# Output projection of the first attention: both row scalings on ScalarE, longer lags between the steps, the weight transposed inside the same stage

## The chip, the cores and the metric

The kernel runs on one core of a Trainium2 chip. The metric is the device time of one execution in microseconds (us). The core has five instruction streams that matter here: TensorE (PE: matmuls and transposes), VectorE (DVE), ScalarE (ACT), GpSimd (POOL) and SyncE (SP, which only issues DMAs here). Each runs its own list of instructions in order and waits for the others through semaphores. TensorE writes to PSUM; in this kernel GpSimd reads and writes SBUF alone.

## The reference, cut to what matters

Two transformer layers on an input of 2 x 1024 rows of 512. Each attention and each feed-forward is wrapped in the same way:

```python
def _layernorm(x, axis=-1, eps=1e-05):
    m = jnp.mean(x, axis=axis, keepdims=True)
    v = jnp.var(x, axis=axis, keepdims=True)
    return (x - m) / jnp.sqrt(v + eps)
...
    x = x + _layernorm(_L0_attn_ref(_layernorm(x, axis=-1), ...), axis=-1)
    x = x + _layernorm(_L0_ffn_ref(_layernorm(x, axis=-1), ...), axis=-1)
```

The change is at the end of the first attention. What is computed there, for 2048 rows: `y = out @ Wo.T` (the last line of the attention), `x1 = x0 + layernorm(y)`, and then `layernorm(x1)`, transposed, as the operand of the feed-forward.

## The kernel before

The program is a row of stages, and each stage is a block with one instruction list per engine and a barrier at its end. The stage in question, `project_residual_norm` (tiles named `l0o_...`), follows the attention (`l0a_...`) and a small stage of its own that transposes the weight Wo (`transpose_weights`, tiles `l0ot_...`). After it comes the first feed-forward (`f0f_...`).

`transpose_weights` takes Wo, already in SBUF (`raw`, shown as `l_raw`), through TensorE in 16 transposes of 128x128 (L133). ScalarE copies each of the four banks out, rounded to fp32r (the high part, L141), and VectorE writes the remainder (the low part, L151). High and low part together keep fp32's precision with three matmuls in place of one: high x high, high x low, low x high (`THREE`).

`project_residual_norm` then works on 16 tiles of 128 rows. For each tile t:

- ScalarE casts the attention's output to its high part (L403), and GpSimd subtracts to get the low part (L475).
- TensorE does y(t): 12 matmuls into a PSUM bank (L378), 4 blocks of the inner dimension times the three pairs.
- VectorE takes the row statistics of y (bn_stats L425, bn_aggr L430), ScalarE the square root (L397), VectorE the reciprocal (L435) and **the first row scaling**, (y - mean) * rstd, from PSUM to the tile z (L463).
- GpSimd adds the residual x0 (L482), and SyncE stores z as x1 (L362).
- VectorE takes the statistics of z, ScalarE the root, VectorE the reciprocal and **the second row scaling** from z to xn (L443).
- TensorE transposes xn in 4 pieces, below called T(t) (L386); ScalarE copies the bank out as the high part (L415) and VectorE the low part (L451), into `x_xT`, the operand of the feed-forward.

What sets the order is written out by hand: each engine runs a loop over steps i, and in step i it does each kind of work for the tile that lags by a fixed number. Before: T(i-5) and y(i) on TensorE; on VectorE second scaling of i-4, statistics of z of i-3, low part of i-6, statistics of y of i, first scaling of i-1. The rings `z`, `ybank`, `tbank` and `ot_hl` hold 4 tiles and `xn` holds 2, and waits guard their reuse. The Python loops are unrolled, so the program's order is the order in the code.

SyncE first issues two loads of x0 and six of the feed-forward's first weights, and then a store per tile.

Of the kernel before, what the change touches and what calls it, by code (L numbers as in the profile page):

```python
# [326 lines left out]
def project_residual_norm(nc, m, ident, tiles, src, dst, oT, WoT_hl, xT_hl, loads):  # L327
# [7 lines left out]
    xn = m.sb("xn", [P, 2, D])  # L335
    ot_hl = m.sb("ot_hl", [P, RING, 2, KT, P], F32R)
    stats, mv = m.sb("stats", [P, 2, RING, 6]), m.sb("mv", [P, 2, RING, 2])
    std, rstd = m.sb("std", [P, 2, RING]), m.sb("rstd", [P, 2, RING])
# [8 lines left out]
    stats_done, mv_done, std_done, rstd_done = ([m.sem(f"{n}{i}") for i in range(2)] for n in (  # L347
        "stats_done", "mv_done", "std_done", "rstd_done"))
    with nc.Block() as block:
# [20 lines left out]
        def _(pe):  # L370
            for i in range(tiles + 5):
# [19 lines left out]
        def _(act):  # L391
# [27 lines left out]
        @block.vector
        def _(dve):  # L420
            nc.vector.memset(eps[:, :], EPS_LN).then_inc(eps_set, 1)

# [9 lines left out]
            def inverse(which, t):  # L432
# [3 lines left out]
                dve.wait_ge(rstd_done[which], t + 1)  # L436

            for i in range(tiles + 6):
                if 0 <= i - 4 < tiles:
                    t, r = i - 4, (i - 4) % RING  # L440
                    inverse(1, t)
                    wait(dve, turned, t - 1)
                    nc.vector.tensor_scalar(xn[:, t % 2, :], z[:, r, :], mv[:, 1, r, 0:1], rstd[:, 1, r:r + 1],  # L443
                                            ALU.subtract, ALU.mult).then_inc(normed, 1)
                if 0 <= i - 3 < tiles:
                    dve.wait_ge(sum_done, i - 2)
                    statistics(1, i - 3, z[:, (i - 3) % RING, :])
                if 0 <= i - 6 < tiles:
                    t = i - 6
# [2020 lines left out]
```

## Time and profile before

| | us |
|---|---|
| median of 3 runs | 3204.28 |
| lowest and highest | 3202.85, 3204.48 |
| the profiled execution | 3199.93 |
| its span | 3198.2 |
| stage l0ot, first transpose to last low part | 632.75 to 637.74 |
| stage l0o, first matmul to last low part | 640.43 to 719.50 |

The profiled execution took 3199.93 us, of which the span of its instructions is 3198.2; it is 4.35 us below the median of the runs. The two stages take about 87 us of it, or 2.7%. All positions in the trace are in us from the span's start. A row of the timeline gives the start, the length, the engine and line, the operation with the tiles it writes and reads, how many of them are merged, and in brackets how long the engine had been idle and what ended that. An instruction of one engine can begin before the last has ended, so a loop's cost is read from start to start.

### The profile page before, as it was taken

How to read it: one execution, taken by the hardware profiler on the slowest of the kernel's cores; microseconds unless marked ns; L12 is line 12 of the kernel's file. 1: busy time of each engine (PE TensorE's matmuls, PEld its weight loads, DVE VectorE, ACT ScalarE, POOL GpSimd, SP SyncE). 2: the span in 40 equal slices, each digit the busy share in tenths (PEclk: the TensorE clock that was granted, in tenths of full speed). 3: DMA queues.
4: the chain of work that ended last, by engine and by line, in shares of the span. 5: the costliest groups of instructions: out<-in, count | busy, mean ns of one | idle time of the engine just before them, and what ended most of it. 6: DMA issues, size and time to landing. Idle time of an engine off the chain costs nothing. (4 is left out here: it accounts for less than half of the span.)

```text
span 3198.2 us, 42777 instructions
## 1 busy us (share of the span) xinstructions
PE 2861.6 (89%) x14636; PEld 2287.2 (72%) x14636; DVE 1894.0 (59%) x3604; ACT 1210.8 (38%) x2334; POOL 992.9 (31%) x780
## 2 busy tenths in 40 slices
PE   7969999779999999458899999857999999499998
PEld 5846666557787878347788888746888888378886
DVE  5647788584453545445566666655666666654446
ACT  2226666532221212133344444322444444243334
POOL 1217877655554636304100000033000000122223
PEclk9979999889999999779999999979999999799999
DMA  4774444142121201671100000040000000300012
GB/s 163 241 210 143 120 128 130 39 144 80 47 63 41 64 24 35 203 283 70 40 23 23 34 23 34 10 159 29 24 23 34 23 23 30 125 20 21 10 36 79
DMA packets 138034, 244.06 MB, mean 76 GB/s; under 512 B 14416, under 2 KB 78928, under 8 KB 137392
## 3 DMA queue, kind: packets, MB, share of 16 engines
q1 hardware_dynamic: 137904, 242.40, 23.2%
q8 instruction: 73, 1.20, 0.2%
q14 instruction: 57, 0.47, 0.0%
HBM read 162.92 MB, written 79.17 MB: 76 GB/s over the span
## 5 line engine op out<-in xcount | busy, mean ns | idle before, releaser
L1071 POOL TENSOR_TENSOR l0a_probs_hl<-l0a_probs,l0a_probs_hl 128x896 fp32r<-128x896 f32 (+1 forms) x128 | 285.3, 2249 | 107.3 <-ACT l0a_probs L999 107.3
L1329 ACT ACTIVATE l1a_probs<-l1a_scores,l1a_row 128x128 f32<-128x128 f32 (+7 forms) x256 | 189.7, 742 | 317.4 <-DVE l1a_row L1366 317.4
L1303 PE MATMUL l1a_obank<-l1a_pT_hl,l1k_v_hl 128*128 128x512 f32 (+3 forms) x1152 | 300.2, 369 | 7.1 <-DVE l1a_pT_hl L1376 7.1
L1376 DVE TENSOR_TENSOR l1a_pT_hl<-l1a_work,l1a_pT_hl 128x512 fp32r<-128x512 f32 (+3 forms) x384 | 213.1, 555 | 154.4 <-ACT l1a_pT_hl L1336 154.2
L1419 POOL TENSOR_TENSOR l1a_q_stage<-l1k_qpe,l1a_ones 128x512 fp32r<-128x512 f32 x32 | 33.4, 1043 | 872.4 <-PE l1a_work L1311 816.7
L1283 PE MATMUL l1a_scores<-l1k_kT_hl,l1a_qa_hl 128*128 128x512 f32 (+3 forms) x1152 | 291.1, 361 | 1.5 <-ACT l1a_probs L1329 1.5
L1336 ACT CAST l1a_pT_hl<-l1a_work 128x512 fp32r<-128x512 f32 (+3 forms) x384 | 183.7, 478 | 105.7 <-PE l1a_work L1294 104.5
L1311 PE MATMUL l1a_work<-l1a_wov,l1a_oT_hl 128*128 128x512 f32 x768 | 214.2, 401 | 5.0 <-DVE l1a_oT_hl L1395 3.0
L1366 DVE TENSOR_REDUCE l1a_row<-l1a_scores 128x1 f32<-128x128 f32 (+7 forms) x256 | 189.8, 751 | 44.0 <-PE l1a_scores L1286 43.9
L1390 DVE SCALAR_TENSOR_TENSOR l_acc<-l1a_work,l1a_row,l_acc 128x512 f32<-128x512 f32 x256 | 189.4, 750 | 34.1 <-PE l1a_work L1311 24.5
L1690 PE MATMUL f0f_ybank<-f0f_wT,f0f_h_hl 128*128 128x512 f32 x768 | 196.5, 406 | 12.6 <-POOL f0f_h_hl L1856 12.5
L1283 PEld LDWEIGHTS l1a_scores<-l1k_kT_hl,l1a_qa_hl 128*128 128x128 f32 x1152 | 188.1, 190 | 21.7 <-ACT l1a_probs L1329 1.8
L1283 PE MATMUL l1a_scores<-l1k_kpe,l1a_q_stack 128*128 128x512 f32 (+3 forms) x768 | 203.1, 346 | 0.0
L1303 PEld LDWEIGHTS l1a_obank<-l1a_pT_hl,l1k_v_hl 128*128 128x128 f32 x1152 | 181.4, 191 | 28.8 <-DVE l1a_pT_hl L1376 14.8
L1294 PE MATMUL l1a_work<-all_ident,l1a_probs 128*128 128x128 f32 x1152 | 191.8, 275 | 9.5 <-DVE l1a_qa_hl L1381 6.1
L1680 PE MATMUL f0f_gbank<-x_xT,f0f_wT 128*128 128x512 f32 x768 | 192.1, 399 | 1.4 <-DVE f0f_wT L1761 1.4
L1680 PE MATMUL f0f_ubank<-x_xT,f0f_wT 128*128 128x512 f32 x768 | 189.3, 395 | 0.0
L1767 DVE TENSOR_TENSOR f0f_hid<-f0f_silu,f0f_ubank 128x512 f32<-128x512 f32 x64 | 44.0, 688 | 229.4 <-PE f0f_ubank L1680 207.4
L1690 PEld LDWEIGHTS f0f_ybank<-f0f_wT,f0f_h_hl 128*128 128x128 f32 x768 | 145.2, 194 | 44.4 <-issue 9.2
L998 ACT ACTIVATE l0a_probs_hl<-l0a_sbank 128x896 fp32r<-128x896 f32 (+1 forms) x128 | 124.5, 972 | 135.3 <-PE l0a_sbank L964 77.9
L1294 PEld LDWEIGHTS l1a_work<-all_ident,l1a_probs 128*128 128x128 f32 x1152 | 140.3, 140 | 47.8 <-DVE l1a_qa_hl L1381 12.8
L1680 PEld LDWEIGHTS f0f_gbank<-x_xT,f0f_wT 128*128 128x128 f32 x768 | 145.8, 190 | 36.7 <-DVE f0f_wT L1761 1.6
(254 smaller groups left out, 6191.0 us busy)
## 6 DMA issues: line engine op xcount, KB each, us to landing
v_dram<-l0f_v_rows SPq DMA_DIRECT2D x24, 768.0 KB, 4.0
qk_dram<-l0f_stage SPq DMA_DIRECT2D x128, 128.0 KB, 2.5
l1a_wov<-wov_dram SPq DMA_DIRECT2D x32, 512.0 KB, 3.4
l0a_v_stage<-v_dram SPq DMA_DIRECT2D x32, 384.0 KB, 4.3
l1a_wabs<-wabs_dram SPq DMA_DIRECT2D x32, 384.0 KB, 3.9
l0a_q_stack<-qk_dram SPq DMA_DIRECT2D x32, 256.0 KB, 3.6
l0a_k_stack<-qk_dram SPq DMA_DIRECT2D x32, 256.0 KB, 3.9
f0f_chunk<-in_L_ffn_w_gate_up SPq DMA_DIRECT2D x32, 256.0 KB, 2.7
```

Source lines behind the costliest of these rows:

```text
L1071: nc.gpsimd.tensor_tensor(probs_hl[:, r, 1, 0:wide], probs[:, r, 0:wide], f32(probs_hl[:, r, 0, 0:wide]), ALU.subtract).then_inc(low_done, 1)
L1283: last = pe.matmul(scores[:, buf, cols], lhs, rhs, start=(i == 0), stop=(not diagonal and i == len(steps) - 1))
L1294: last = pe.transpose(work[:, slot, i * P:(i + 1) * P], probs[s][:, first + n, :], ident[:, :])
L1303: last = pe.matmul(obank[:, c:SPAN], src["v_hl"][:, a, n, :], pT_hl[:, ring(n, s), b, c:SPAN], start=(n == 0 and i == 0), stop=(n == QT * ...
L1311: last = pe.matmul(work[:, slot, :], oT_hl[:, s, a, n * P:(n + 1) * P], wov[:, hp, b, :], start=(i == 0), stop=(i == 2))
L1329: nc.scalar.activation(probs[s][:, first:first + wide, :].rearrange("p k c -> p (k c)"), scores[:, n % S_AHEAD, 0:wide * P], ACT.Exp, bias ...
L1336: nc.scalar.copy(pT_hl[:, ring(n, s), 0, c:SPAN], work[:, slot, c:SPAN]).then_inc(turned_high, 1)
L1366: nc.vector.tensor_reduce(row[:, 0, row_slot:row_slot + 1], scores[:, n % S_AHEAD, 0:wide * P], AX.X, ALU.max, negate=True).then_inc(max_d ...
L1376: nc.vector.tensor_tensor(pT_hl[:, r, 1, c:SPAN], work[:, slot, c:SPAN], f32(pT_hl[:, r, 0, c:SPAN]), ALU.subtract).then_inc(work_free[slo ...
L1390: nc.vector.scalar_tensor_tensor(out=out[:, t, :], in0=work[:, slot, :], scalar=row[:, 2, row_slot:row_slot + 1], in1=out[:, t, :], op0=AL ...
L1680: last = pe.matmul(bank[:, b, :], wT[:, half, wa, w, c * HG + b * P:c * HG + (b + 1) * P], xT_hl[:, xa, c, a * SPAN:(a + 1) * SPAN], start ...
L1690: last = pe.matmul(ybank[:, b % 2, :], h_hl[:, a % 2, ht, ha, b * P:(b + 1) * P], wT[:, half, wa, 2, ht * D:(ht + 1) * D], start=(n == 0), ...
```

## The change

- The stage `l0ot` is gone. Its 16 transposes, 4 casts and 4 subtractions stand at the begin of `l0o`, behind the first three casts of the attention's output on ScalarE. They use the first four uses of `tbank`, which is why the counts of `turned`, `high_done` and `low_done` start at `KT` (4). The weight's tile moves from `l_WoT` to `l0o_WoT_hl`.
- Both row scalings are now ScalarE's, as `Identity(scale * in + bias)` with scale = rstd and bias = -mean * rstd. For that bias VectorE computes a `shift` (128x1) after each reciprocal.
- The lags are longer: T(i-7) in place of T(i-5); the low part of xT at i-9 in place of i-6; the residual sum at i-2 in place of i-1; the second scaling at i-6 in place of i-4.

```diff
@@ class of work on TensorE @@
+            for k in range(KT):
+                for o in range(KT):
+                    last = pe.transpose(tbank[:, k, o * P:(o + 1) * P], raw[:, o, k * P:(k + 1) * P], ident[:, :])
+                last.then_inc(turned, 1)
+            pe.wait_ge(low_done, KT)
-            for i in range(tiles + 5):
+            for i in range(tiles + 7):
...
-                if i >= 5:
-                    t = i - 5
+                if i >= 7:
+                    t = i - 7
                     pe.wait_ge(normed, t + 1)
-                    wait(pe, low_done, t - RING + 1)
+                    pe.wait_ge(low_done, KT + t - RING + 1)
@@ ScalarE @@
+            def scaled(which, t, to, rows):
+                r = t % RING
+                act.wait_ge(shift_done[which], t + 1)
+                return nc.scalar.activation(to, rows, ACT.Identity, bias=shift[:, which, r:r + 1],
+                                            scale=rstd[:, which, r:r + 1])
...
+            for k in range(KT):
+                act.wait_ge(turned, k + 1)
+                nc.scalar.copy(WoT_hl[:, 0, k, :], tbank[:, k, :]).then_inc(high_done, 1)
+            for i in range(tiles + 8):
+                if 0 <= i - 5 < tiles:
+                    root(1, i - 5)
                 if 0 <= i - 1 < tiles:
                     root(0, i - 1)
                 if 0 <= i - 6 < tiles:
                     t = i - 6
-                    act.wait_ge(turned, t + 1)
+                    act.wait_ge(turned, KT + t - 1)
+                    scaled(1, t, xn[:, t % 2, :], z[:, t % RING, :]).then_inc(normed, 1)
+                if 0 <= i - 8 < tiles:
+                    t = i - 8
+                    act.wait_ge(turned, KT + t + 1)
                     nc.scalar.copy(xT_hl[:, 0, :, t * P:(t + 1) * P],
...
+                if 0 <= i - 2 < tiles:
+                    t, r = i - 2, (i - 2) % RING
+                    wait(act, stored[r], 16 * (t // RING))
+                    wait(act, normed, t - RING + 1)
+                    scaled(0, t, z[:, r, :], ybank[:, r, :]).then_inc(z_done, 1)
                 high(i + 3)
@@ VectorE @@
+            for i in range(tiles + 9):
+                if 0 <= i - 5 < tiles:
+                    inverse(1, i - 5)
...
+                    statistics(1, i - 4, z[:, (i - 4) % RING, :])
+                if i < tiles:
+                    dve.wait_ge(y_full, i + 1)
+                    statistics(0, i, ybank[:, i % RING, :])
+                if 0 <= i - 4 < tiles:
+                    aggregate(1, i - 4)
+                if 0 <= i - 1 < tiles:
+                    inverse(0, i - 1)
+                if 0 <= i - 9 < tiles:
...
                 if i < tiles:
                     aggregate(0, i)
@@ GpSimd @@
-                if 0 <= i - 1 < tiles:
-                    t = i - 1
+                if 0 <= i - 2 < tiles:
+                    t = i - 2
```

VectorE's list, one tile in the middle of the stage, before (L443 is the second scaling, L463 the first, L451 the low part of xT):

```order
L443 TENSOR_SCALAR l0o_xn<-l0o_z,l0o_mv,l0o_rstd 128x512
L425 BN_STATS l0o_stats<-l0o_z 128x6
L451 TENSOR_TENSOR x_xT<-l0o_tbank,x_xT 128x4x128
L430 BN_AGGR l0o_mv<-l0o_stats 128x2
L425 BN_STATS l0o_stats<-l0o_ybank 128x6
L435 RECIPROCAL l0o_rstd<-l0o_std 128x1
L463 TENSOR_SCALAR l0o_z<-l0o_ybank,l0o_mv,l0o_rstd 128x512
L430 BN_AGGR l0o_mv<-l0o_stats 128x2
L435 RECIPROCAL l0o_rstd<-l0o_std 128x1
```

VectorE's list, one tile in the middle of the stage, of the changed kernel (L465 is the new shift):

```order
L463 RECIPROCAL l0o_rstd<-l0o_std 128x1
L465 SCALAR_TENSOR_TENSOR l0o_shift<-l0o_mv,l0o_rstd 128x1
L453 BN_STATS l0o_stats<-l0o_z 128x6
L453 BN_STATS l0o_stats<-l0o_ybank 128x6
L458 BN_AGGR l0o_mv<-l0o_stats 128x2
L463 RECIPROCAL l0o_rstd<-l0o_std 128x1
L465 SCALAR_TENSOR_TENSOR l0o_shift<-l0o_mv,l0o_rstd 128x1
L485 TENSOR_TENSOR x_xT<-l0o_tbank,x_xT 128x4x128
L458 BN_AGGR l0o_mv<-l0o_stats 128x2
```

The two operations on 128x512 are gone from it and two on 128x1 have come; the low part of xT stands late in the step.

ScalarE's list, one tile in the middle of the stage, before (two roots, the copy of xT, the cast of the next attention tile):

```order
L397 ACTIVATE l0o_std<-l0o_mv,l0o_eps 128x1 x2
L415 CAST x_xT<-l0o_tbank 128x4x128
L403 CAST l0o_ot_hl<-l_oT 128x512
L397 ACTIVATE l0o_std<-l0o_mv,l0o_eps 128x1 x2
L415 CAST x_xT<-l0o_tbank 128x4x128
```

ScalarE's list of the changed kernel, the same place:

```order
L403 ACTIVATE l0o_std<-l0o_mv,l0o_eps 128x1 x2
L409 ACTIVATE l0o_xn<-l0o_z,l0o_shift,l0o_rstd 128x512
L434 CAST x_xT<-l0o_tbank 128x4x128
L409 ACTIVATE l0o_z<-l0o_ybank,l0o_shift,l0o_rstd 128x512
L415 CAST l0o_ot_hl<-l_oT 128x512
```

Both scalings stand between the roots and the cast for tile i+3, one on each side of the copy of xT.

The begin of the changed stage on ScalarE, up to the first scaling:

```order
L415 CAST l0o_ot_hl<-l_oT 128x512 x3
L421 CAST l0o_WoT_hl<-l0o_tbank 128x512 x4
L415 CAST l0o_ot_hl<-l_oT 128x512
L403 ACT_TABLE_LOAD
L403 ACTIVATE l0o_std<-l0o_mv,l0o_eps 128x1
L415 CAST l0o_ot_hl<-l_oT 128x512
L403 ACTIVATE l0o_std<-l0o_mv,l0o_eps 128x1
L409 ACTIVATE l0o_z<-l0o_ybank,l0o_shift,l0o_rstd 128x512
```

The weight's four casts stand behind three of the attention's output, in the same block; the load of the activation table (ACT_TABLE_LOAD) is the only one of the stage, as it was before.

## Rows read from the trace of the kernel before

**Rows 1.** Busy time in two stretches; the first row names the columns.
```profile
core 0: us, PE busy (x) PEld busy (x) DVE busy (x) ACT busy (x) POOL busy (x), PEclk, DMA share, GB/s
642.00:643.00 1.00, 1.00 (x4) 0.80 (x3) 0.00 (x0) 0.00 (x0) 1.00 (x2) 0.50 1.00 352
700.00:720.00 20.00, 5.45 (x23) 3.37 (x21) 17.86 (x38) 5.49 (x14) 3.79 (x3) 0.62 0.14 52
```

**Rows 2.** Waits, 640 to 720: total us, times, longest.
```profile
PE l0o_tbank L386 <- DVE l0o_xn L443: 15.0, 13, 3.7
PE l0o_ybank L378 <- POOL l0o_ot_hl L475: 7.5, 9, 4.0
```

**Rows 3.** Timeline of VectorE, one tile: start, length, operation.
```profile
667.12 1.48 DVE L443 TENSOR_SCALAR l0o_xn<-l0o_z,l0o_mv,l0o_rstd 128x512 f32<-128x512 f32 x1
668.52 0.68 DVE L425 BATCH_NORM_STATS2 l0o_stats<-l0o_z 128x6 f32<-128x512 f32 x1
669.12 0.67 DVE L451 TENSOR_TENSOR x_xT<-l0o_tbank,x_xT 128x512 fp32r<-128x512 f32 x1
669.71 0.17 DVE L430 BATCH_NORM_AGGREGATE l0o_mv<-l0o_stats 128x2 f32<-128x6 f32 x1
669.80 0.66 DVE L425 BATCH_NORM_STATS2 l0o_stats<-l0o_ybank 128x6 f32<-128x512 f32 x1
670.38 0.14 DVE L435 RECIPROCAL l0o_rstd<-l0o_std 128x1 f32<-128x1 f32 x1
670.56 0.81 DVE L463 TENSOR_SCALAR l0o_z<-l0o_ybank,l0o_mv,l0o_rstd 128x512 f32<-128x512 f32 x1
671.29 0.17 DVE L430 BATCH_NORM_AGGREGATE l0o_mv<-l0o_stats 128x2 f32<-128x6 f32 x1
...
671.55 1.48 DVE L443 TENSOR_SCALAR l0o_xn<-l0o_z,l0o_mv,l0o_rstd 128x512 f32<-128x512 f32 x1
```

**Rows 4.** Timeline: the second scaling with GpSimd idle; four casts of GpSimd with VectorE idle.
```profile
716.44 0.55 DVE L443 TENSOR_SCALAR l0o_xn<-l0o_z,l0o_mv,l0o_rstd 128x512 f32<-128x512 f32 x1
...
639.11 4.99 POOL L475 TENSOR_TENSOR l0o_ot_hl<-l_oT,l0o_ot_hl 128x512 fp32r<-128x512 f32 x4 [6.87 <-ACT l0o_ot_hl L403]
```

**Rows 5.** Timeline of TensorE: the weight's transposes, the first y, a step, y(15).
```profile
632.75 3.65 PE L133 MATMUL l0ot_bank<-all_ident,l_raw 128*128 128x128 f32 x16 [12.67 <-PEq L836]
640.43 17.93 PE L378 MATMUL l0o_ybank<-l_WoT,l0o_ot_hl 128*128 128x512 f32 x72 [4.03 <-POOL l0o_ot_hl L475]
...
661.39 0.60 PE L386 MATMUL l0o_tbank<-all_ident,l0o_xn 128*128 128x128 f32 x4
661.74 3.02 PE L378 MATMUL l0o_ybank<-l_WoT,l0o_ot_hl 128*128 128x512 f32 x12
664.60 0.60 PE L386 MATMUL l0o_tbank<-all_ident,l0o_xn 128*128 128x128 f32 x4
...
696.38 3.02 PE L378 MATMUL l0o_ybank<-l_WoT,l0o_ot_hl 128*128 128x512 f32 x12 [0.47 <-POOL l0o_ot_hl L475]
```

**Rows 6.** Timeline of ScalarE: a step here, and the same Identity in the last stage.
```profile
675.93 0.29 ACT L397 ACTIVATE l0o_std<-l0o_mv,l0o_eps 128x1 f32<-128x1 f32 x1 [1.29 <-DVE l0o_mv L430]
676.14 0.57 ACT L415 CAST x_xT<-l0o_tbank 128x512 fp32r<-128x512 f32 x1
676.60 0.62 ACT L403 CAST l0o_ot_hl<-l_oT 128x512 fp32r<-128x512 f32 x1
...
3183.09 0.30 ACT L1734 ACTIVATE f1f_root<-f1f_var,f1f_eps 128x4 f32<-128x4 f32 x1 [0.58 <-DVE f1f_var L1812]
3183.82 2.94 ACT L1739 ACTIVATE f1f_z<-f_acc,f1f_shift,f1f_rstd 128x512 f32<-128x512 f32 x4 [0.44 <-DVE f1f_shift L1820]
```

**Rows 7.** Timeline of VectorE: last weight low part, last of xT, a shift elsewhere.
```profile
637.05 0.69 DVE L151 TENSOR_TENSOR l_WoT<-l0ot_bank,l_WoT 128x512 fp32r<-128x512 f32 x1 [0.16 <-ACT l_WoT L141]
...
718.81 0.69 DVE L451 TENSOR_TENSOR x_xT<-l0o_tbank,x_xT 128x512 fp32r<-128x512 f32 x1 [0.63 <-ACT x_xT L415]
...
3190.48 0.16 DVE L1820 SCALAR_TENSOR_TENSOR f1f_shift<-f1f_mv,f1f_rstd 128x4 f32<-128x4 f32 x1
```

More of the change, by code:

```diff
@@ L324, in _, with project_residual_norm @@
                 nc.gpsimd.tensor_tensor(z[:, r, :], z[:, r, :], x[:, t % (2 * QT), :], ALU.add).then_inc(sum_done, 1)
-def project_residual_norm(nc, m, ident, tiles, src, dst, oT, WoT_hl, xT_hl, loads):
+def project_residual_norm(nc, m, ident, tiles, src, dst, oT, raw, xT_hl, loads):
     RING = 4
@@ L335, in project_residual_norm @@
     xn = m.sb("xn", [P, 2, D])
+    WoT_hl = m.sb("WoT_hl", [P, 2, KT, D], F32R)
     ot_hl = m.sb("ot_hl", [P, RING, 2, KT, P], F32R)
     stats, mv = m.sb("stats", [P, 2, RING, 6]), m.sb("mv", [P, 2, RING, 2])
-    std, rstd = m.sb("std", [P, 2, RING]), m.sb("rstd", [P, 2, RING])
+    std, rstd, shift = (m.sb(n, [P, 2, RING]) for n in ("std", "rstd", "shift"))
     eps = m.sb("eps", [P, 1])
@@ L406, in _ @@
                 high(t)
-            for i in range(tiles + 6):
-                if 0 <= i - 4 < tiles:
-                    root(1, i - 4)
+            for k in range(KT):
[4 more added lines that the diff above has]
+                    root(1, i - 5)
                 if 0 <= i - 1 < tiles:
@@ L421, in _ @@
             nc.vector.memset(eps[:, :], EPS_LN).then_inc(eps_set, 1)
+            for k in range(KT):
+                dve.wait_ge(high_done, k + 1)
+                nc.vector.tensor_tensor(WoT_hl[:, 1, k, :], tbank[:, k, :], f32(WoT_hl[:, 0, k, :]), ALU.subtract
+                                        ).then_inc(low_done, 1)
             def statistics(which, t, y):
@@ L436, in inverse @@
                 dve.wait_ge(rstd_done[which], t + 1)
-            for i in range(tiles + 6):
-                if 0 <= i - 4 < tiles:
[L440 to L449, printed above, removed]
-                    dve.wait_ge(high_done, t + 1)
+                nc.vector.scalar_tensor_tensor(out=shift[:, which, r:r + 1], in0=mv[:, which, r, 0:1], scalar=-1.0,
+                                               in1=rstd[:, which, r:r + 1], op0=ALU.mult, op1=ALU.mult
+                                               ).then_inc(shift_done[which], 1)
+            for i in range(tiles + 9):
+                if 0 <= i - 5 < tiles:
+                    inverse(1, i - 5)
+                if 0 <= i - 4 < tiles:
+                    dve.wait_ge(sum_done, i - 3)
+                    statistics(1, i - 4, z[:, (i - 4) % RING, :])
[7 more added lines that the diff above has]
+                if 0 <= i - 9 < tiles:
+                    t = i - 9
+                    dve.wait_ge(high_done, KT + t + 1)
                     nc.vector.tensor_tensor(xT_hl[:, 1, :, t * P:(t + 1) * P],
@@ L453, in _ @@
                                             f32(xT_hl[:, 0, :, t * P:(t + 1) * P]), ALU.subtract).then_inc(low_done, 1)
-                if 0 <= i - 3 < tiles:
-                    aggregate(1, i - 3)
-                if i < tiles:
-                    dve.wait_ge(y_full, i + 1)
-                    statistics(0, i, ybank[:, i % RING, :])
-                if 0 <= i - 1 < tiles:
-                    t, r = i - 1, (i - 1) % RING
-                    inverse(0, t)
-                    wait(dve, stored[r], 16 * (t // RING))
-                    nc.vector.tensor_scalar(z[:, r, :], ybank[:, r, :], mv[:, 0, r, 0:1], rstd[:, 0, r:r + 1],
-                                            ALU.subtract, ALU.mult).then_inc(z_done, 1)
                 if i < tiles:
                     aggregate(0, i)
-            dve.wait_ge(low_done, tiles)
+            dve.wait_ge(low_done, KT + tiles)
         @block.gpsimd
         def _(pool):
-            for i in range(-2, tiles + 1):
+            for i in range(-2, tiles + 2):
                 if i + 2 < tiles:
```

10 lines of the change are left out of this document (3 added, 7 removed).

## Prediction

> **What bounds the kernel now.** The page's slices say that TensorE is the busiest engine of the whole, so I first asked whether it is so in the stage that is changed. The waits of that stretch say no: TensorE waits 15.0 us for the second scaling and 7.5 us for the low part of the attention's output [rows 2]. VectorE's timeline shows why: one tile takes 671.55 - 667.12 = 4.43 us, with no idle time in any row [rows 3]. TensorE's own step, where nothing held it, is 664.60 - 661.39 = 3.21 us: 0.35 for a T and 2.86 for a y [rows 5]. So VectorE sets the pace here and TensorE is next. Three stretches are to be read separately: the begin (last transpose of the weight to the first matmul), the sixteen y, and the tail, from the end of y(15) at 696.38 + 3.02 = 699.40 to the last low part at 718.81 + 0.69 = 719.50. The tail is 20.1 us in which TensorE does only small transposes (5.45 us busy of 20) and VectorE is nearly full (17.86) [rows 1].
>
> **The begin.** The 16 transposes still start when the attention ends, near 632.75, and take 3.65 us [rows 5]; nothing of the new stage lets them start earlier. In the way of ScalarE stand three casts of 0.62 [rows 6], together 1.9 us, which end near 634.6; the fourth bank is only full at 636.4, so the last weight cast is not moved, nor the last low part, which ends at 637.05 + 0.69 = 637.74 [rows 7]. TensorE can then start y(0), near 637.8, since GpSimd has made its low part (1.25 us [rows 4]) by about 635. Before, y(0) started at 640.43 [rows 5], because a barrier, a cast and a GpSimd pass stood in between. Gain: **2.6 us**. SyncE's eight loads start some 5 us earlier, beside nothing else. The clock: before, TensorE had run its first matmuls at a granted 0.50, which is 1.2 GHz, and still at 642 to 643 [rows 1], 2.6 us from the first, worth 1.3 us. After, its pause is 1.4 us and not 4.0. I assume the same slow start; if the clock is up sooner, up to 1.3 us more.
>
> **The pace.** Per tile, from start to start:
>
> VectorE keeps two statistics (0.60 and 0.58), the low part (0.59), two aggregates (0.09 each), two reciprocals (0.18 each) [rows 3]: 2.31. It gains two shifts. The nearest row is one of 128x4, 0.16 [rows 7]; with overlap 0.1, at most 0.18. Sum 2.5 (at most 2.7). What leaves is 1.40 and 0.73, less the 0.2 for the shifts.
>
> ScalarE keeps two roots (0.21), the copy of xT (0.46), and the cast (0.62, say 0.55 where another follows) [rows 6]. It gains two Identities. The trace has the very instruction in the last stage: four in 2.94 us, or (2.94 - 0.80) / 3 = 0.71 from start to start, 0.80 alone [rows 6]. It reads SBUF there, while one of the two reads PSUM here; copies cost 0.57 from PSUM and 0.62 from SBUF, so I take 0.80 for both. Sum: 0.42 + 1.42 + 0.46 + 0.55 = **2.85**. Without any overlap: 0.58 + 1.60 + 0.57 + 0.62 = 3.37. There is no new table load: in the last stage a root is followed by Identities with none in between [rows 6], and the changed list has a single one.
>
> GpSimd: a cast at 1.25 (4.99 for four [rows 4]) and a sum of the same shape, taken alike: 2.5, far from the bound too.
>
> The second scaling takes 1.48 while GpSimd works and 0.55 when it doesn't [rows 3, 4], so the move frees more of VectorE than it costs ScalarE. The Trainium skill speaks against the move: in "ScalarE: Activation LUTs", section "Rules for kernel authors", adding and multiplying belong on VectorE, which it calls up to about 3 times faster in bf16. By the row with GpSimd idle that would hold (0.55 against 0.80), by the row beside GpSimd it doesn't; and a rule for one operation doesn't say which engine sets the pace.
>
> So TensorE is next, at 3.21. Do the new waits let it run? Call Y(i) the end of y(i). VectorE ends its step i about 1.9 behind Y(i) (statistics, reciprocal and shift, low part, two aggregates). ScalarE's step i+1 begins there and takes 2.65 more from its second root, to Y(i) + 4.5. TensorE needs z free for y(i+3) (the scaling of tile i-1, done by Y(i) + 4), which is due at Y(i) + 6.4 or later, and xn of tile i-5 for the T behind y(i+2), due at Y(i) + 6.4, done at Y(i) + 3. Each has over 2 us to spare. The steps of VectorE and ScalarE depend on each other over two steps: ScalarE 2.65, a root 0.35, VectorE 2.5, in all 5.5 for two tiles, 2.75 for one. TensorE holds.
>
> The sixteen y: the first six as before, 17.93 (with the slow clock); y(6) and y(7) at 2.86; eight steps of 3.21 for the rest. Sum 17.9 + 5.7 + 25.7 = 49.3, in place of 699.40 - 640.43 = 58.97. Gain: **9.7 us**. With ScalarE at 3.37 for the last eight it is 1.3 less.
>
> **The tail.** Followed for tile 15, from its y full: VectorE's step 1.8; ScalarE root, Identity, copy, Identity of tile 14 (2.1), then root, Identity, copy (1.4): the first scaling of tile 15 begins at 5.3 and ends at 6.1. GpSimd's sum to 7.4. VectorE is in a low part until 8.4; statistics and aggregate to 9.2. Root; the Identity of tile 14 and a copy (1.4); VectorE's reciprocal and shift lie beside them. The second scaling of tile 15 begins at 10.6 and ends at 11.4; four transposes at the slow clock, about 1.1, to 12.5; copy 0.6, low part 0.7: **14.0 us**. Gain 20.1 - 14.0 = **6.1 us**. The longer lags add no time of their own, because a step without y is cheap. With no overlap of neighbours each piece grows by a tenth or two, some 2 us less gain; if ScalarE reaches tile 15 earlier than I let it, 1.5 more.
>
> **Sum.** 2.6 + 9.7 + 6.1 = 18.4 us. The profiled execution goes from 3199.93 to 3181.5. The median of the runs stands 4.35 above it, and I carry that over: 3204.28 - 18.4 = 3185.9. The next stage is only moved: its weights are issued at the begin of this stage and are there long before.
>
> **Rivals.**
>
> *ScalarE becomes the bound.* Its list grows from under half full to 89% (2.85 of 3.21), with six waits in a step. For it: the nearest rows leave 0.36 a tile. Against: most semaphores are long up. At 3.6 a tile over the ten tiles from y(6) on, the pace loses 10 x 0.39 = 3.9 of its gain and keeps 5.8; the tail keeps 4.5: with the begin 12.9 us, 3191.4.
>
> *The clock is up early.* 1.3 us more: 3184.6.
>
> *Lockstep, slower than before.* ScalarE's root for tile i-1 waits for the last instruction of VectorE's step i-1, and VectorE's step i begins with a wait for a root. If the two took turns rather than ran beside each other, a tile would take 2.85 + 2.5 = 5.35; sixteen, 85.6 us in place of 59, a loss of 27, less 2.6 and what is left of the tail's gain: about +20, 3224. It decides from about (59 + 2.6 + 6.1) / 16 = 4.2 a tile. Against it: the roots stand first in ScalarE's step, so VectorE is released while ScalarE's long part runs.
>
> *The gain is given back.* The next stage would have to wait for something that doesn't move, such as a weight load. SyncE issues those before the tiles, so there is next to nothing for it. Result within 6 us of before.
>
> **Chances.** TensorE's pace with a clock as before: 0.70. ScalarE the bound: 0.14. Clock early: 0.08. Given back: 0.05. Lockstep: 0.03. The measurement tells a difference of about 0.2%, 6.4 us. Faster 0.92, same 0.05, slower 0.03. The range reaches from the early clock and a tail shorter by 1.5 with a us for the scatter of the runs (3182) to the case with ScalarE as the bound and half a us of scatter (3192).
>
> **What would show it.** Right: y(0) near 637.8; T to T 3.2 us with TensorE without a wait in the middle; VectorE idle a fifth of each tile; Identity 0.80 or less; last low part near 701. If the second scaling was slow because of GpSimd, GpSimd's casts in the middle of the stage take what they take at its begin with VectorE idle, 1.25 [rows 4]. (The Trainium skill, "SBUF — State Buffer", section "Who interferes with whom", names one exclusive pair of ports for the two engines; no term above needs it.) **Wrong:** T to T of 3.5 with TensorE waiting for xn or z (ScalarE), over 4.2 (lockstep), Identity from PSUM well over 0.8, a tail over 16, or y(0) at 640.

## The result, and the profile after

The changed kernel took 3187.83 us in the median of 5 runs (3182.02 to 3191.39), the kernel before 3204.28 (3202.57 to 3207.29 in 5). The medians lie 16.5 us or 0.5% apart. The ratio on record is 0.9941, with a 95% interval of 0.9930 to 0.9952, which is 15 to 22 us faster. The forecast was 3185.9, in a range of 3182 to 3192. The interval holds both the 18.4 us that were forecast and the 16.5 of the medians, so the whole time can't tell them apart.

The profiled execution took 3187.83 us with a span of 3186.0, 12.2 us below that of before; 18.4 was forecast against that one. Where the two meet and differ is read in the stage. TensorE's timeline of the changed kernel, to be held against [rows 5]:

```profile
633.10 3.65 PE L374 MATMUL l0o_tbank<-all_ident,l_raw 128*128 128x128 f32 x16 [12.79 <-PEq L859]
638.15 23.77 PE L384 MATMUL l0o_ybank<-l0o_WoT_hl,l0o_ot_hl 128*128 128x512 f32 x96 [1.40 <-DVE l0o_WoT_hl L448]
...
668.18 0.60 PE L392 MATMUL l0o_tbank<-all_ident,l0o_xn 128*128 128x128 f32 x4
668.53 3.00 PE L384 MATMUL l0o_ybank<-l0o_WoT_hl,l0o_ot_hl 128*128 128x512 f32 x12
671.38 0.60 PE L392 MATMUL l0o_tbank<-all_ident,l0o_xn 128*128 128x128 f32 x4
...
684.84 3.02 PE L384 MATMUL l0o_ybank<-l0o_WoT_hl,l0o_ot_hl 128*128 128x512 f32 x12
```

y(0) stands 638.15 - 633.10 = 5.05 us behind the first transpose (7.68 before). From T to T it is 3.20 us, with no wait in brackets: TensorE sets the pace. (One step of the eight, from 674.59 to 678.08, took 3.49.) y(15) ends at 687.86. VectorE's last low parts (three merged) end at 703.06:

```profile
701.05 2.01 DVE L485 TENSOR_TENSOR x_xT<-l0o_tbank,x_xT 128x512 fp32r<-128x512 f32 x3 [0.50 <-ACT x_xT L434]
```

| us | before | forecast | after |
|---|---|---|---|
| begin, first transpose to y(0) | 7.68 | 5.1 | 5.05 |
| the sixteen y | 58.97 | 49.3 | 49.71 |
| tail, y(15) to the last low part | 20.10 | 14.0 | 15.20 |
| stage | 86.75 | 68.4 | 69.96 |

The stage gave 16.8 us of the 18.4 forecast. What is short, 1.6 us, is in the y and the tail. VectorE's timeline shows an instruction that I had priced at 0.16 us; GpSimd's timeline of the same moment follows it.

```profile
667.35 0.12 DVE L463 RECIPROCAL l0o_rstd<-l0o_std 128x1 f32<-128x1 f32 x1
667.51 1.05 DVE L465 SCALAR_TENSOR_TENSOR l0o_shift<-l0o_mv,l0o_rstd 128x1 f32<-128x1 f32 x1
668.49 0.17 DVE L458 BATCH_NORM_AGGREGATE l0o_mv<-l0o_stats 128x2 f32<-128x6 f32 x1
668.58 0.12 DVE L463 RECIPROCAL l0o_rstd<-l0o_std 128x1 f32<-128x1 f32 x1
668.74 1.08 DVE L465 SCALAR_TENSOR_TENSOR l0o_shift<-l0o_mv,l0o_rstd 128x1 f32<-128x1 f32 x1
```

```profile
667.25 1.29 POOL L505 TENSOR_TENSOR l0o_z<-l0o_z,l0o_x 128x512 f32<-128x512 f32 x1 [1.13 <-ACT l0o_z L409]
668.50 1.29 POOL L498 TENSOR_TENSOR l0o_ot_hl<-l_oT,l0o_ot_hl 128x512 fp32r<-128x512 f32 x1
```

The shift, one element per row, takes 1.05 and 1.08 us. Its ends, 668.56 and 669.82, lie 0.02 and 0.03 behind the ends of GpSimd's instructions, 668.54 and 669.79. Reciprocals of the same size beside the same GpSimd work take 0.12. Of the 32 shifts 20 started while GpSimd was at work, and all of them end within 0.03 us of the end of its instruction; the 12 that met it idle took 0.16. The groups of the stage, ordered by cost (busy us and mean ns behind the bar), put it together:

```profile
L505 POOL TENSOR_TENSOR l0o_z<-l0o_z,l0o_x 128x512 f32<-128x512 f32 x16 | 20.5, 1284 | 15.6 <-ACT l0o_z L409 15.6
L498 POOL TENSOR_TENSOR l0o_ot_hl<-l_oT,l0o_ot_hl 128x512 fp32r<-128x512 f32 x16 | 20.5, 1289 | 7.1 <-ACT l0o_ot_hl L415 7.1
L465 DVE SCALAR_TENSOR_TENSOR l0o_shift<-l0o_mv,l0o_rstd 128x1 f32<-128x1 f32 x32 | 17.6, 551 | 1.1
L409 ACT ACTIVATE l0o_xn<-l0o_z,l0o_shift,l0o_rstd 128x512 f32<-128x512 f32 x16 | 12.8, 801 | 0.0
L409 ACT ACTIVATE l0o_z<-l0o_ybank,l0o_shift,l0o_rstd 128x512 f32<-128x512 f32 x16 | 12.4, 775 | 0.2
```

Thirty-two shifts cost 17.6 us of VectorE's time in place of 5. GpSimd's casts and sums are at 1.29 each, or 1.25 from start to start, as at the begin of the stage (the casts in the middle were near 1.45 before), and the Identities at 0.80 from SBUF and 0.78 from PSUM.

### The profile page after: what moved, and what is told of

Its sections match the earlier page's. It is cut to its first block and busy times, and to the rows that moved or that the text cites. A ratio compares the mean times of both kernels' runs of the same rounds, so it can differ in the third digit from the quotient of the medians.

```text
span 3186.0 us, 42804 instructions
## 1 busy us (share of the span) xinstructions
PE 2862.2 (90%) x14636; PEld 2289.0 (72%) x14636; DVE 1879.3 (59%) x3604; ACT 1231.7 (39%) x2366; POOL 990.2 (31%) x780
```

## The experiments

Each stage time below is read as in the table above, from the first transpose of the weight to the last low part of xT, in the profiled execution; it depends little on the rest of the kernel, unlike the whole time. Whole times are medians, and ratios are against the kernel before, run on the same chip. One thing differs between the profiles that the edits don't explain: in four of the twelve (the lags alone, the scalings alone, only the second scaling, the reciprocal later) TensorE's granted clock was already 1.00 at the first y; in the others it was at half then and came up later. Here are the four and then, for comparison, the changed kernel and the run with only the first scaling, each in a stretch of 1 us early in the first y.

```profile
639.00:640.00 1.00, 1.00 (x6) 0.82 (x5) 0.00 (x0) 0.60 (x1) 0.66 (x1) 1.00 1.06 383
636.00:637.00 1.00, 1.00 (x6) 0.83 (x5) 0.00 (x0) 0.18 (x1) 0.24 (x1) 1.00 1.03 389
637.00:638.00 1.00, 1.00 (x5) 0.84 (x5) 0.00 (x0) 0.84 (x1) 0.91 (x1) 1.00 1.04 406
637.00:638.00 1.00, 1.00 (x6) 0.77 (x6) 0.00 (x0) 0.47 (x1) 0.53 (x1) 1.00 1.01 381
```

```profile
639.00:640.00 1.00, 1.00 (x3) 0.73 (x3) 0.00 (x0) 0.19 (x1) 0.24 (x1) 0.50 0.94 313
637.00:638.00 1.00, 1.00 (x4) 0.71 (x4) 0.00 (x0) 0.59 (x1) 0.64 (x1) 0.50 0.97 356
```

The granted clock is third from the end. In all twelve it was up before the first y was full, so what it costs lies ahead of VectorE's statistics: VectorE's first statistics of y start 3.0 to 3.1 us behind the start of y(0) in the four and 4.4 to 5.3 in the others. So stage times are compared across the two groups from those first statistics to the last low part; a table at the end of this section has both lengths.

**The weight alone.** The kernel before with the transposes, casts and subtractions of the weight at the begin of the stage.

```diff
+            for k in range(KT):
+                for o in range(KT):
+                    last = pe.transpose(tbank[:, k, o * P:(o + 1) * P], raw[:, o, k * P:(k + 1) * P], ident[:, :])
+                last.then_inc(turned, 1)
+            pe.wait_ge(low_done, KT)
             for i in range(tiles + 5):
...
-                with phase("l0ot") as m:
-                    transpose_weights(nc, m, ident, square_jobs(raw, WoT, 0, -1), [])
```

> The kernel before with one edit: the weight is transposed inside the projection's stage; scalings and lags as before. My theory: the begin is worth the 2.6 us that the trace of after shows between the first transpose and y(0) (7.68 to 5.05) and nothing else changes: VectorE stays at 4.43 us a tile, the stage goes from 86.8 us (first transpose of the weight to last low part) to 84.1, the time falls by 2 to 3 us. Rival: the earlier begin is taken back, because VectorE sets the pace: then the stage stays near 86.8.

Begin 5.05, y 59.12, tail 20.14: stage 84.31, so 2.4 us less. The time was 3202.06 (before 3202.50), ratio 0.9994 (0.9984 to 1.0004), which tells no difference of this size. The begin gives its own length and nothing else; VectorE's pace is the old one.

**Everything but the weight.** The changed kernel with the weight in its own stage.

```diff
-            for k in range(KT):
-                for o in range(KT):
-                    last = pe.transpose(tbank[:, k, o * P:(o + 1) * P], raw[:, o, k * P:(k + 1) * P], ident[:, :])
-                last.then_inc(turned, 1)
-            pe.wait_ge(low_done, KT)
...
+                with phase("l0ot") as m:
+                    transpose_weights(nc, m, ident, square_jobs(raw, WoT, 0, -1), [])
```

> The changed kernel with the weight transposed in its own stage as before; scalings on ScalarE and long lags kept. If the parts add up, the two stages together take 70.0 + 2.6 = 72.6 us, y(0) starts 7.7 us after the first transpose, the sixteen y take 49 to 50 us and the tail 15; time 14 us below before. If the early begin matters for more than itself (clock, loads), the sum is off by 1.5 us or more.

Begin 7.67, y 49.96, tail 15.23: 72.86, within 0.3 of the sum of parts. From the first statistics it takes 60.18 us, and the changed kernel 60.16. The time was 3190.37, ratio 0.9952 (0.9939 to 0.9965). The parts add up.

**The lags alone.** The changed kernel with both scalings on VectorE, at the changed kernel's lags. The order inside VectorE's step is the changed kernel's too, with the low part of xT late in it, so this run changes lags and order together.

```diff
                 if 0 <= i - 5 < tiles:
                     inverse(1, i - 5)
+                if 0 <= i - 6 < tiles:
+                    t, r = i - 6, (i - 6) % RING
+                    dve.wait_ge(turned, KT + t - 1)
+                    nc.vector.tensor_scalar(xn[:, t % 2, :], z[:, r, :], mv[:, 1, r, 0:1], rstd[:, 1, r:r + 1],
+                                            ALU.subtract, ALU.mult).then_inc(normed, 1)
...
                 if 0 <= i - 1 < tiles:
                     inverse(0, i - 1)
+                if 0 <= i - 2 < tiles:
+                    t, r = i - 2, (i - 2) % RING
...
+                    nc.vector.tensor_scalar(z[:, r, :], ybank[:, r, :], mv[:, 0, r, 0:1], rstd[:, 0, r:r + 1],
+                                            ALU.subtract, ALU.mult).then_inc(z_done, 1)
```

> The changed kernel (weight inside the stage, long lags) with both scalings back on VectorE at the same lags, and no shift. My theory: VectorE sets the pace as before, 4.2 to 4.5 us a tile from T to T, TensorE waits for VectorE's results; stage 83 to 90 us. Rival: the longer lags alone brought the pace, by taking waits out: 3.2 to 3.5 a tile and a stage near 70.

My theory missed: 3.83 us from T to T and a stage of 77.44 (begin 5.05, y 52.14, tail 20.25); 3196.07, ratio 0.9976 (0.9966 to 0.9986). VectorE still sets the pace, as its timeline of this run shows, but the second scaling takes 0.89 there and not 1.48. Below it is GpSimd's, and then the sum of GpSimd that the scaling at 667.12 of the kernel before met.

```profile
675.23 0.81 DVE L479 TENSOR_SCALAR l0o_z<-l0o_ybank,l0o_mv,l0o_rstd 128x512 f32<-128x512 f32 x1
675.96 0.69 DVE L484 TENSOR_TENSOR x_xT<-l0o_tbank,x_xT 128x512 fp32r<-128x512 f32 x1
676.55 0.18 DVE L449 BATCH_NORM_AGGREGATE l0o_mv<-l0o_stats 128x2 f32<-128x6 f32 x1
676.64 0.14 DVE L454 RECIPROCAL l0o_rstd<-l0o_std 128x1 f32<-128x1 f32 x1
676.81 0.89 DVE L463 TENSOR_SCALAR l0o_xn<-l0o_z,l0o_mv,l0o_rstd 128x512 f32<-128x512 f32 x1
```

```profile
676.12 1.29 POOL L504 TENSOR_TENSOR l0o_z<-l0o_z,l0o_x 128x512 f32<-128x512 f32 x1 [1.10 <-DVE l0o_z L479]
677.37 1.49 POOL L497 TENSOR_TENSOR l0o_ot_hl<-l_oT,l0o_ot_hl 128x512 fp32r<-128x512 f32 x1
```

```profile
667.03 1.29 POOL L482 TENSOR_TENSOR l0o_z<-l0o_z,l0o_x 128x512 f32<-128x512 f32 x1 [1.70 <-DVE l0o_z L463]
```

Before, the scaling of xn followed 0.18 us behind the end of the scaling of z, which starts GpSimd's sum, so it met nearly the whole sum [rows 3]. In this order a low part lies between them, and 0.6 us of the sum is left when it starts. The run shows this inside itself. Its first four second scalings stand before the first low part of xT, directly behind the first scaling, and take 1.48 to 1.49; from the fifth on a low part lies between, and they take 0.88 or 0.89 for as long as there are y:

```profile
668.56 1.48 DVE L463 TENSOR_SCALAR l0o_xn<-l0o_z,l0o_mv,l0o_rstd 128x512 f32<-128x512 f32 x1
...
672.13 0.68 DVE L484 TENSOR_TENSOR x_xT<-l0o_tbank,x_xT 128x512 fp32r<-128x512 f32 x1
...
672.99 0.88 DVE L463 TENSOR_SCALAR l0o_xn<-l0o_z,l0o_mv,l0o_rstd 128x512 f32<-128x512 f32 x1
```

VectorE's step stays at 3.83 us as the low part comes in: its 0.60 is what the scaling no longer waits. So the 0.6 us that a tile gained against the 4.43 before come from the place of the low part in VectorE's step. What the longer lags add with the scalings on VectorE wasn't measured apart from that.

**The scalings alone.** The changed kernel, weight inside, with the lags of before. The low part stays late in VectorE's step.

```diff
-                if 0 <= i - 6 < tiles:
-                    t = i - 6
+                if 0 <= i - 4 < tiles:
+                    t = i - 4
                     act.wait_ge(turned, KT + t - 1)
                     scaled(1, t, xn[:, t % 2, :], z[:, t % RING, :]).then_inc(normed, 1)
...
-                if 0 <= i - 2 < tiles:
-                    t, r = i - 2, (i - 2) % RING
+                if 0 <= i - 1 < tiles:
+                    t, r = i - 1, (i - 1) % RING
```

> The changed kernel (weight inside, scalings on ScalarE) with the lags of before: T(i-5), low part at i-6, sum at i-1, second scaling at i-4, first scaling at i-1. My theory: ScalarE's first scaling of i-1 then waits for a shift that VectorE makes near the end of its own step, and VectorE's next step waits for a root that stands behind it: the two engines take turns, 4.2 to 4.7 us a tile, stage 82 to 90 us, no better than with the weight alone. Rival: the lags don't matter, 3.2 a tile, and fewer steps in the tail make the stage 67 to 70 us.

3.80 us from T to T, stage 77.04 (begin 5.04, y 53.45, tail 18.55); 3190.17, ratio 0.9957 (0.9941 to 0.9972). The mechanism is there, the size was too large. The waits between 655 and 690 of this run (total us, times, longest) show that ScalarE and VectorE wait for each other in each tile:

```profile
POOL l0o_z L505 <- ACT l0o_z L409: 11.5, 9, 1.3
DVE l0o_rstd L463 <- ACT l0o_std L403: 8.5, 9, 1.5
PEld l0o_tbank L392 <- ACT l0o_xn L409: 7.3, 9, 0.8
ACT l0o_xn L409 <- DVE l0o_shift L465: 5.8, 9, 1.1
PE l0o_tbank L392 <- ACT l0o_xn L409: 3.5, 9, 0.4
ACT l0o_z L409 <- DVE l0o_shift L465: 3.1, 10, 0.7
```

So neither of the two gives the pace of 3.2 alone. Read from the first statistics, the 74.7 us of the weight alone become 69.3 with the lags (and the new order) and 68.9 with the scalings, so each alone is worth 5.4 to 5.8 us, and together they are worth 14.5, more than their sum. Between this run and the changed kernel, with the order the same, the longer lags are worth 68.9 - 60.2 = 8.7 us. (The stage times 77.4 and 77.0 flatter both by the 1.5 us of the early clock.)

**One scaling each.** The changed kernel with only the second scaling on ScalarE, and with only the first; the other is on VectorE, in the form of the run with the lags alone.

```diff
@@ only the second on ScalarE @@
...
-                    scaled(0, t, z[:, r, :], ybank[:, r, :]).then_inc(z_done, 1)
...
+                if which != 1:
+                    return
...
@@ only the first on ScalarE @@
...
-                    scaled(1, t, xn[:, t % 2, :], z[:, t % RING, :]).then_inc(normed, 1)
...
+                if which != 0:
+                    return
...
```

> The changed kernel with only the second scaling (xn) on ScalarE; the first (z from PSUM, 0.81 us) is on VectorE at the same lag, and one shift is left. VectorE: 2.31 + 0.73 + a shift of 0.1 to 0.9 = 3.1 to 3.9 a tile. Theory: the second scaling was the one worth moving, as it was held by GpSimd: pace 3.2 to 3.5 (lags alone gave 3.83), stage 70 to 75. Rival: both moves are needed, pace above 3.6.

> The changed kernel with only the first scaling (z) on ScalarE; the second (xn) is on VectorE and one shift is left. VectorE: 2.31 + 0.55 to 1.40 + a shift of 0.1 to 0.9 = 3.0 to 4.6 a tile. Theory: 3.5 to 4.0 a tile, close to the 3.83 of the lags alone, because the shift and the scaling both wait for GpSimd; stage 75 to 79. Rival: the two moves are worth the same, and this one runs at the pace of the other.

Only the second: 3.56 from T to T, stage 74.29, 3189.43 (ratio 0.9957, 0.9941 to 0.9973). Only the first: 3.2 up to T(4) and 3.6 to 4.1 behind it, stage 76.30, 3190.24 (0.9963, 0.9950 to 0.9975). Both stages lie in the ranges expected, the first near its upper end (its pace of 3.56 is just above the 3.5), the second near its lower. But they can't be compared as they stand, since the clock was up early in the first and not in the second. From the first statistics they take 66.26 and 66.34 us, against 69.33 with both scalings on VectorE and 60.16 with none. So each move alone is worth about 3 us, and both 9.2: for the whole stage the rival that I had put to the second run, that the two moves are worth the same, holds. In the steady part the second is worth more (3.56 a tile against 3.77); the first makes up for it before T(4). The single shift left waits as well, 0.62 us in the median in the one and 0.89 in the other.

**GpSimd's sum in one column.** The kernel before, where GpSimd adds the residual in the first column alone.

```diff
-                    nc.gpsimd.tensor_tensor(z[:, r, :], z[:, r, :], x[:, t % (2 * QT), :], ALU.add).then_inc(sum_done, 1)
+                    nc.gpsimd.tensor_tensor(z[:, r, 0:1], z[:, r, 0:1], x[:, t % (2 * QT), 0:1], ALU.add
+                                            ).then_inc(sum_done, 1)
```

> The kernel before with one edit that changes what is computed: GpSimd adds the residual x0 in the first of the 512 columns alone, so its sum is short (x1 and all that follows lack x0 in the others). Theory: the second scaling on VectorE took 1.48 us in the stage because GpSimd's sum ran beside it; with the sum gone it takes 0.54 to 0.7 where GpSimd is idle, VectorE's step falls from 4.43 to 3.5 to 3.7, and the y take 52 to 54 us. Rival: the 1.48 is the price of that instruction in this place (its operands or the one before it), and it stays over 1.3.

The y took 60.30 us where I expected 52 to 54, and the one execution 3196.97 us. I had asked for the scaling to be fast "where GpSimd is idle" and overlooked that GpSimd isn't: its next cast moves up into the gap. VectorE's row, then GpSimd's:

```profile
681.02 1.60 DVE L443 TENSOR_SCALAR l0o_xn<-l0o_z,l0o_mv,l0o_rstd 128x512 f32<-128x512 f32 x1
```

```profile
681.07 1.27 POOL L475 TENSOR_TENSOR l0o_ot_hl<-l_oT,l0o_ot_hl 128x512 fp32r<-128x512 f32 x1
```

The scaling started 0.05 us ahead of the cast and ended 0.28 behind its end (682.62 against 682.34). In the middle of the stage the step even grew, to 4.55 us from T to T. (Another 0.9 us of the y stand before T(0), where TensorE's clock was at half for longer.) But the casts end with tile 15, and then neither of GpSimd's large instructions is left: VectorE still does both scalings and takes 3.49 us for a step (T at 696.32, 699.80, 703.29), where it took 4.40 before, and the second scaling takes 0.55:

```profile
699.20 0.55 DVE L443 TENSOR_SCALAR l0o_xn<-l0o_z,l0o_mv,l0o_rstd 128x512 f32<-128x512 f32 x1
```

Before, GpSimd's sum still ran there, so this pair has one difference. The 0.9 us is GpSimd's; the scaling waits for whichever of GpSimd's instructions it meets.

**The shift in another form.** The changed kernel with a tensor_scalar, which takes rstd as a per-row scalar and reads one tensor.

```diff
-                nc.vector.scalar_tensor_tensor(out=shift[:, which, r:r + 1], in0=mv[:, which, r, 0:1], scalar=-1.0,
-                                               in1=rstd[:, which, r:r + 1], op0=ALU.mult, op1=ALU.mult
-                                               ).then_inc(shift_done[which], 1)
+                nc.vector.tensor_scalar(shift[:, which, r:r + 1], mv[:, which, r, 0:1], rstd[:, which, r:r + 1], -1.0,
+                                        ALU.mult, ALU.mult).then_inc(shift_done[which], 1)
```

> The changed kernel with the shift computed by a tensor_scalar (mean times the per-row scalar rstd times -1: one tensor read from SBUF) in place of the scalar_tensor_tensor, which reads two. In the trace of after that one took 551 ns in the mean (up to 1.17 us), and its end falls on the end of a GpSimd instruction. Theory A: an instruction of VectorE with two inputs from SBUF waits for GpSimd's running one; then the mean falls to 0.13 to 0.20 us, VectorE's step to 2.5 us, TensorE's pace stays 3.21 (it sets it), the 0.3 us stall in the middle goes, the tail falls from 15.2 to 14.0 to 14.6; stage 68.4 to 69.2 us, time 1 us below after. Theory B: every VectorE instruction that follows a reciprocal there is held: the mean stays near 0.5 and nothing changes.

The row of the tile (least, median and most ns) is without a wait in any of the 32:

```profile
L465 DVE TENSOR_SCALAR l0o_shift<-l0o_mv,l0o_rstd x32: 212/214/216, 647.3 to 698.3; 128x1 f32<-128x1 f32 x32
```

Alone it is dearer than the old form (0.21 against 0.16), and it is never held. Begin 5.05, y 49.22, tail 13.91: stage 68.18. 3186.19, ratio 0.9944 (0.9930 to 0.9958), not to be told from the changed kernel by the whole time; the stage is 1.8 us shorter, 1.6 of it behind the first statistics and 0.2 in the clock before them. Between 662 and 688 VectorE was busy for 20.00 us of 26, and in the changed kernel for 25.15:

```profile
662.00:688.00 26.00, 26.00 (x131) 21.49 (x130) 20.00 (x71) 22.17 (x47) 18.95 (x15) 1.00 0.41 142
```

```profile
662.00:688.00 26.00, 25.95 (x131) 21.24 (x130) 25.15 (x72) 21.63 (x46) 19.39 (x16) 1.00 0.38 135
```

Theory A holds, with one thing left open: the edit changes the operation and the number of its inputs from SBUF at once. That two inputs alone are not enough the low part of xT shows, a tensor_tensor with one input in PSUM and one in SBUF, which takes 0.66 to 0.69 us in the changed kernel whether GpSimd works beside it or not.

**The reciprocal later.** On top of that, VectorE's step with the second scaling's reciprocal behind the aggregate.

```diff
             for i in range(tiles + 9):
-                if 0 <= i - 5 < tiles:
-                    inverse(1, i - 5)
...
                 if 0 <= i - 4 < tiles:
                     aggregate(1, i - 4)
+                if 0 <= i - 5 < tiles:
+                    inverse(1, i - 5)
```

> As the run with the tensor_scalar shift, and in VectorE's step the reciprocal and shift of the second scaling stand behind the statistics and aggregate of z rather than before them. In the tail of after, a step takes 2.0 us, as a root, a reciprocal, a shift, the statistics, an aggregate and the next root stand in one chain. Without the first three in it a step is 1.5 to 1.7: tail 12.5 to 13.5 us, stage 67 to 68 us, time 1.5 to 3 us below after. If ScalarE's own list (root, Identity, copy: 1.4) or the sum of z bounds the tail instead, nothing beyond the shift's part is gained.

Begin 4.84, y 47.72, tail 13.66: stage 66.22; 3184.90, ratio 0.9944 (0.9930 to 0.9958). The tail is only 0.25 us shorter, above the 12.5 to 13.5 expected: the other case of the expectation holds, that ScalarE's own list bounds it. ScalarE's timeline shows no wait in it: a step with an Identity for z takes 2.03 us and one without 1.37, and that list is now the bound.

```profile
688.58 0.80 ACT L409 ACTIVATE l0o_xn<-l0o_z,l0o_shift,l0o_rstd 128x512 f32<-128x512 f32 x1
689.29 0.57 ACT L434 CAST x_xT<-l0o_tbank 128x512 fp32r<-128x512 f32 x1
689.75 0.78 ACT L409 ACTIVATE l0o_z<-l0o_ybank,l0o_shift,l0o_rstd 128x512 f32<-128x512 f32 x1
690.43 0.29 ACT L403 ACTIVATE l0o_std<-l0o_mv,l0o_eps 128x1 f32<-128x1 f32 x1
690.61 0.81 ACT L409 ACTIVATE l0o_xn<-l0o_z,l0o_shift,l0o_rstd 128x512 f32<-128x512 f32 x1
```

The other 1.5 us, in the y, aren't the edit's (from the first statistics the two runs take 58.28 and 58.55). Busy time in stretches of 1 us, with the granted clock third from the end: the first y of this run, and then the first of the changed kernel.

```profile
636.00:637.00 1.00, 0.52 (x2) 0.47 (x3) 0.43 (x1) 0.98 (x2) 0.96 (x2) 1.00 1.02 363
```

```profile
640.00:641.00 1.00, 1.00 (x4) 0.78 (x3) 0.00 (x0) 0.00 (x0) 0.00 (x0) 0.50 1.05 408
641.00:642.00 1.00, 1.00 (x4) 0.77 (x3) 0.00 (x0) 0.00 (x0) 0.00 (x0) 0.59 1.08 412
```

The instructions up to there are the same in both, and the clock was up (1.00, 2.4 GHz) at the first y in one execution and at half for over 3 us in the other. That is the rival of the early clock, worth 1.5 us. Nine kernels of the study have the same instructions up to the first y, with the weight inside the stage; in the one profile that there is of each, four had the clock up and five had it at half for another 3.1 to 4.0 us. So it is not a property of one kernel, and why an execution falls on one side stays open.

**Two scalings back in the tail.** On top of that, the first scaling of tiles 14 and 15 at the end of VectorE's step.

```diff
...
+                if tiles - 2 <= i - 1 < tiles:
+                    t, r = i - 1, (i - 1) % RING
+                    wait(dve, stored[r], 16 * (t // RING))
+                    wait(dve, normed, t - RING + 1)
+                    dve.wait_ge(z_done, t)
+                    nc.vector.tensor_scalar(z[:, r, :], ybank[:, r, :], mv[:, 0, r, 0:1], rstd[:, 0, r:r + 1],
+                                            ALU.subtract, ALU.mult).then_inc(z_done, 1)
...
```

ScalarE's list ends its first scalings two tiles earlier, and these two tiles need no shift.

> The run with the tensor_scalar shift and the later reciprocal, and for the last two tiles the first scaling is on VectorE, at the end of its step, since VectorE is half idle in the tail while ScalarE's steps with an Identity for z take 2.04 us and those without 1.37. Theory: ScalarE bounds the tail; without the two Identities it shrinks from 13.7 to 11.5 to 12.5 us, stage 66 to 67 us (68 to 69 less the gain) where the clock is up at its usual point. Rival: the wait goes to VectorE's low parts or TensorE's slow transposes, and the tail stays above 13.

It missed, and in the direction that I had put as the rival: begin 5.04, y 49.14, tail 16.01, stage 70.19; 3186.11, ratio 0.9946 (0.9932 to 0.9961). VectorE's timeline shows the two scalings held:

```profile
689.21 0.81 DVE L496 TENSOR_SCALAR l0o_z<-l0o_ybank,l0o_mv,l0o_rstd 128x512 f32<-128x512 f32 x1 [1.13 <-issue]
...
692.13 0.81 DVE L496 TENSOR_SCALAR l0o_z<-l0o_ybank,l0o_mv,l0o_rstd 128x512 f32<-128x512 f32 x1 [0.20 <-ACT l0o_xn L409]
```

z has four places, so z(15) may only be written when xn(11) has read its place, and that is done by ScalarE, in its next step. The profile names this only for the second row, but both start 0.09 us behind the end of such an Identity (689.12 and 692.04). On ScalarE this wait cost nothing, since the Identity for xn stood right ahead of it in the same list; on VectorE the whole step stands behind it.

All twelve profiles, with the clock at the start of the first y:

| kernel | clock at the first y | stage, us | from the first statistics, us |
|---|---|---|---|
| before | half | 86.75 | 74.71 |
| the weight alone | half | 84.31 | 74.70 |
| everything but the weight | half | 72.86 | 60.18 |
| the lags alone | full | 77.44 | 69.33 |
| the scalings alone | full | 77.04 | 68.90 |
| only the second scaling | full | 74.29 | 66.26 |
| only the first scaling | half | 76.30 | 66.34 |
| the changed kernel | half | 69.96 | 60.16 |
| the shift in another form | half | 68.18 | 58.55 |
| the reciprocal later | full | 66.22 | 58.28 |
| two scalings back in the tail | half | 70.19 | 60.65 |
| GpSimd's sum in one column | half | 85.09 | 72.16 |

## Why the prediction was right, and where it was off

**What bounds.** Right: VectorE set the pace of before, and TensorE that of after, with 3.20 us for the 3.21 that I took from its free step. The run with the lags alone adds a correction: 0.93 of VectorE's 4.43 was a meeting with GpSimd, and a mere change of order brings it down to 0.34 (a second scaling of 1.48 and of 0.89, against 0.55 alone).

**The begin.** Forecast 2.6, measured 2.63, with the same 2.6 in the two runs that separate the weight from the rest. The fourth bank of the weight was indeed what the last cast waited for.

**The pace.** 9.7 forecast, 9.26 measured. ScalarE's price was right: 0.71 from start to start by the row in the last stage, 0.80 and 0.78 alone. VectorE's was wrong: "gains two shifts ... 0.16; with overlap 0.1, at most 0.18". They took 0.55 in the mean. VectorE's step was up to 3.67 us (664.91 to 668.58 between reciprocals), more than TensorE's 3.21. It cost little because the longer lags let VectorE fall behind and catch up; at one place TensorE waited 0.3 us. The sign "VectorE idle a fifth of each tile" did not come: between 662 and 688 it was busy for 25.15 us of 26. With the other form of the shift it was idle for 6 of 26.

**The tail.** 6.1 forecast, 4.9 measured. There the shift's wait is on the path. With the other form of the shift the tail was 13.91, against 14.0 in my walk, and the y 49.22 against 49.3. The walk fits that run piece by piece: the last first scaling ends 6.0 us behind y(15) (6.1 in the walk) and the last second scaling begins at 10.6 (10.6). So the walk was right in every term but that one: the term "two shifts" was mis-sized, 0.16 in place of 0.55 us each, which is 1.6 us of the stage.

Why I missed it can be said exactly. The row that I took the price from stands in the last stage, where no GpSimd instruction ran beside it. And I cited the section "Who interferes with whom" of the Trainium skill's "SBUF — State Buffer" for the second scaling, but did not hold the new instruction against it. It also says that a VectorE instruction with two inputs from SBUF contends with a GpSimd instruction that reads SBUF. The shift is such an instruction, GpSimd was busy for 41 us of the stage, and the runs with the shift in either form agree with the rule: 20 of 32 held in the one, none of 32 in the other.

**The rest of the kernel.** The stage gave 16.8 us and the profiled span 12.2. The stage began 0.35 us later, and from the last low part to the end of the span it was 2478.7 us before and 2482.9 after. In the ten other profiles of the study that stretch, whose instructions are the same, takes 2477.8 to 2489.2, and the stage's own begin lies between 630.10 and 638.10. The 4.2 us are thus no larger than what the same instructions differ by over these profiles, and the median of five runs, 16.5 below, agrees with the stage's 16.8. That they are no cost of the change is likely but not shown: the four profiles with the lags of before lie at 2477.8 to 2478.7 us, the eight with the longer lags at 2480.1 to 2489.2, and no run looks for a reason. The forecast of the whole time was off by 1.9 us, 1.6 of it in the stage; that the rest came out so small is luck, with medians that scatter by more.

**The rivals.** ScalarE didn't become the bound: it waited 13.9 us for VectorE's statistics between 645 and 700, and only in the run with the later reciprocal is it the tail's. The early clock was not in the changed kernel's profile, but in four others', at about the price given (1.3 forecast, 1.5 to 1.9 measured). Four of the nine kernels with the weight inside had it, so the chance of 0.08 looks too low. Lockstep doesn't show with the long lags; with the short ones it is there, at 3.80 a tile, below the 4.2 from which it would have made a loss. Nothing was given back.

## What to carry to other kernels

Before pricing an instruction by a row from another stage, look at what the other engines did beside that row, GpSimd above all; an instruction of one element per row took 0.16 us there and up to 1.17 here. When a scaling moves from VectorE to ScalarE, make its bias with a form that reads one tensor from SBUF. Separate lags, order and moves by a run of each: here lags and order were changed together, each half of the change alone gave 5.4 to 5.8 us of 14.5, and what looked like the lags' gain on VectorE's pace was the order's, while with the scalings on ScalarE the lags were worth 8.7 us. And before you compare stage times of two profiles, compare the granted clock at their first matmuls: here it was worth up to 1.9 us, and made two moves of equal worth look like 3.2 and 1.1.

## What was unexpected of the hardware

- A scalar_tensor_tensor on 128x1 with both inputs in SBUF took 0.16 us with GpSimd idle and up to 1171 ns beside it, its end then always within 0.03 us of the end of a GpSimd instruction on 128x512; reciprocal (one input, 0.12 to 0.16) and tensor_scalar with a per-row scalar (0.212 to 0.216) beside the same work were not held.
- The tensor_scalar on 128x512 from SBUF to SBUF, which does meet GpSimd, took 0.54 to 1.63 us over the runs, ending 0.28 or 0.29 us behind the GpSimd instruction that it met, where the rows above show one.
- With equal instructions up to that point, TensorE's granted clock at the first y was 1.00 in four executions and 0.50 in five others.
